# adaLN block with block attention and a routed FFN: q and k projected once per group of tokens, feature matmuls over 32 rows in two row groups

## The reference

```python
mod = silu(c) @ wmod                       # per batch: sa, ca, ga, sb, cb, gb
h = layernorm(x) * (1 + ca) + sa
q, k, v = split(h @ w_qkv.T)               # 8 heads of 16
qp = elu(q_head @ proj[head]) + 1          # 16 -> 128 features per head
kp = elu(k_head @ proj[head]) + 1
kv = kp.T @ v ;  num = qp @ kv             # inside each block of 32 tokens
out = num / (qp . sum(kp) + 1e-8)
x = x + ga * (out @ w_out.T + b_out)       # |ga|, |gb| held at 0.25 or more
h = layernorm(x) * (1 + cb) + sb
e = argmax(softmax(h @ w_red @ wg_n.T))    # one of 8 experts for each token
x = x + gb * score * (gelu(h @ w1[e] + b1[e]) @ w2[e] + b2[e])
```

## Time and profile before

| | value |
|---|---|
| runs (three) | 354.63, 355.92, 356.35 us |
| profiled execution, first to last instruction | 351.6 us |
| what lies around it (median of the runs less the span) | 4.3 us |
| setup until the first Relu of features | 14.59 us |
| step of group 0 | 26.80 us |
| steps of groups 1 and 2 (no scatter) | 20.58 and 21.66 us |
| steps of groups 3 to 6 (with a scatter) | 25.75, 29.95, 28.91, 29.05 us |
| step of group 7, to the end of its features' Exp | 22.23 us |
| tail of the routing | 36.00 us |
| expert stage | 93.08 us |
| busy: PE, ACT, DVE, POOL | 303.9, 217.3, 238.8, 157.1 us |
| mean granted TensorE clock | 0.919 |

### The profile page before, as it was taken

How to read it: one execution, slowest core, us unless ns; L and a number is a source line. 1 busy time by engine, 2 the same in 40 slices (tenths; PEclk the granted TensorE clock), 3 DMA queues, 4 the chain that set the end, 5 groups by cost and what they waited for, 6 DMA issues and landing times. The chain is left out here.

```text
span 351.6 us, 12222 instructions
## 1 busy us (share of the span) xinstructions
PE 303.9 (86%) x4080; PEld 235.6 (67%) x4081; DVE 238.8 (68%) x762; ACT 217.3 (62%) x498; POOL 157.1 (45%) x169
## 2 busy tenths in 40 slices
PE   7887999999799799789979979667869999999970
PEld 3545767777576477567757757343349999999970
DVE  3778689899778548757936958874715666666660
ACT  2478499888678459649837959311116766776740
POOL 6103513534735732661680480575503455455451
PEclk9999699999989859969967999976989999999996
DMA  6993000200220210030040022023942544444400
GB/s 168 333 311 83 0 5 2 62 5 0 85 66 1 90 60 0 35 114 0 0 149 1 2 92 62 4 91 128 281 147 67 143 118 119 131 123 115 144 26 0
DMA packets 23611, 29.53 MB, mean 84 GB/s; under 512 B 2831, under 2 KB 18451, under 8 KB 23584
## 3 DMA queue, kind: packets, MB, share of 16 engines
q1 hardware_dynamic: 19712, 19.98, 20.2%
q0 software_dynamic: 3296, 8.41, 6.6%
q10 hardware_dynamic: 576, 0.79, 0.7%
HBM read 15.32 MB, written 10.64 MB: 74 GB/s over the span
## 5 line engine op out<-in xcount | busy, mean ns | idle before, releaser
L1005 DVE SCALAR_TENSOR_TENSOR phi<-ps,ebuf 128x512 f32<-128x512 f32 x128 | 82.2, 683 | 46.5 <-ACT ebuf L494 45.9
L490 ACT ACTIVATE ebuf<-ps 128x1024 f32<-128x1024 f32 x64 | 65.5, 1024 | 36.1 <-PE ps L682 32.7
L494 ACT ACTIVATE ebuf<-ebuf 128x512 f32<-128x512 f32 x128 | 74.3, 635 | 0.1
L680 PE MATMUL ps<-hT_hi,mix_lo 128*128 (+1 forms) x128 | 63.2, 494 | 9.0 <-DVE phi L1005 5.9
L462 POOL DMA_INDIRECT out<-yo,tok x39 | 40.0, 1025 | 51.3 <-DVE yo L1311 29.0
L593 ACT ACTIVATE gT<-ps,b_cols 128x128 f32<-128x128 f32 x156 | 44.6, 368 | 21.8 <-issue 14.2
L682 PE MATMUL ps<-hT_hi,mix_hi 128*128 (+1 forms) x128 | 54.9, 429 | 0.5 <-issue 0.3
L681 PE MATMUL ps<-hT_lo,mix_hi 128*128 (+1 forms) x128 | 54.8, 428 | 0.0
L835 PE MATMUL ps<-w_sb,gT 128*128 x312 | 41.3, 275 | 0.2 <-ACT gT L593 0.2
L680 PEld LDWEIGHTS ps<-hT_hi,mix_lo 128*128 128x128 f32 x128 | 26.1, 204 | 20.2 <-DVE phi L1005 6.9
L835 PEld LDWEIGHTS ps<-w_sb,gT 128*128 128x128 f32 x312 | 38.0, 192 | 0.4 <-issue 0.4
(11 more groups left out here) (170 smaller groups left out, 476.8 us busy)
## 6 DMA issues: line engine op xcount, KB each, us to landing
rin<-sorted_rows SPq DMA_DIRECT2D x39, 192.5 KB
w1b<-in_L_ffn_w SPq DMA_DIRECT2D x1, 2048.0 KB, 13.7
rec<-h2m SPq DMA_DIRECT2D x7, 256.0 KB, 2.6
rec<-x SPq DMA_DIRECT2D x7, 256.0 KB, 2.8
sorted_rows<-pad_rec SPq DMA_DIRECT2D x5, 192.5 KB
sorted_rows<-pad_rec ACTq DMA_DIRECT2D x4, 192.5 KB
out<-yo,tok POOLq DMA_INDIRECT x39
w1b<-in_L_ffn_b SPq DMA_DIRECT2D x1, 512.0 KB, 6.7
```

The costliest lines, as they stand in the source:

```text
L490: nc.scalar.activation(ebuf[:, h % 2, :, :], x_ps[h % 2], ACT.Relu, scale=-1.0).then_inc(s_neg, 1)
L494: nc.scalar.activation(ebuf[:, h % 2, j, :], ebuf[:, h % 2, j, :], ACT.Exp, scale=-1.0).then_inc(s_exp, 1)
L680: mm(x_ps[h % 2][:, j, :], mix_lo[:, j, h, :], hi, start=True, stop=False)
L1005: v.scalar_tensor_tensor(out=phi[:, h % 4, j, :], in0=x_ps[h % 2][:, j, :], scalar=0.0, in1=ebuf[:, h % 2, j, :], op0=ALU.max, op1=ALU.add ...
```

## The change

Instead of folded weights, q and k are projected once for each group (`project_in`): two fp32 matmuls of 128 rows x 512 tokens with the transposed weights `wqkvT`. Both use the one PSUM bank `t_ps`, one after the other. ScalarE copies each out as the high part in fp32r (`keep_qk_hi`), VectorE subtracts and gives the low part (`split_lo`). GpSimd's `split_lo` and VectorE's `split_hi` go.

The feature matmuls then contract over the 16 values of a head only. A matmul takes the 32 rows of two neighbouring heads; the rows of the other head are zero in `proj_m` (times `parity`). One unit h of the loop now makes q (even h) or k (odd h) features of a pair of heads, (0,2), (1,3), (4,6) or (5,7). The six matmuls of a unit take the two heads in turn, and the two heads of a pair lie in different groups of 32 rows and go to different PSUM banks. A unit waits until both halves of the unit two before it are done; before, each half waited for its own. The scores of two heads are computed together after every second unit, and ScalarE's copy of them is one of 128x256 in place of two of 128x128.

w_qkv, w_red and w_out arrive transposed (and w_out permuted) from the host, so their transposes and copies in the setup go. SP's first load is x of group 0. In TensorE's order `turn_xn` and in ScalarE's `keep_hT` move from h=5 to h=4, `project_in` for q stands at h=5 and for k at h=6. TensorE's loop holds two steps per turn.

```diff
-            fold(0, 0)
-            fold(1, 0)
...
+            def project_in(g, j):
+                if j == 0:
+                    pe.wait_ge(s_ht, g + 1)
+                else:
+                    pe.wait_ge(s_lo, 2 * g + 1)
+                mm(t_ps, wqkvT[:, j, :], hT[:, :], start=True, stop=True).then_inc(s_qk, 1)
...
-                for j in range(2):
-                    if not (isinstance(g, int) and g == 0 and h < 2):
-                        pe.wait_ge(s_phi, 2 * (H * g + h) - 3 + j)
-
-                    mm(x_ps[h % 2][:, j, :], mix_lo[:, j, h, :], hi, start=True, stop=False)
-                    mm(x_ps[h % 2][:, j, :], mix_hi[:, j, h, :], lo, start=False, stop=False)
-                    mm(x_ps[h % 2][:, j, :], mix_hi[:, j, h, :], hi, start=False, stop=True).then_inc(s_x, 1)
+                j, heads = h % 2, PAIRS[h // 2]
+                if h < 2:
+                    pe.wait_ge(s_lo, 2 * g + j + 1)
+                if isinstance(g, int) and g == 0 and h < 2:
+                    pe.wait_ge(set_proj, 1)
+                else:
+                    pe.wait_ge(s_phi, 2 * (H * g + h) - 2)
+                for wt, mv, first, last in ((proj_lo, qk_hi, True, False), (proj_hi, qk_lo, False, False), (proj_hi, qk_hi, False, True)):
+                    for i, head in enumerate(heads):
+                        at = slice((head // 2) * BLK, (head // 2 + 1) * BLK)
+                        done = mm(x_ps[h % 2][:, i, :], wt[at, head % 2, :], mv[at, par, j, :], start=first, stop=last)
+                done.then_inc(s_x, 1)
...
+            def keep_qk_hi(g, j, first):
+                act.wait_ge(s_qk, 2 * g + j + 1)
+                if not first:
+                    act.wait_ge(s_x, H * (g - 1) - 1 + j)
+                nc.scalar.copy(qk_hi[:, bass.ds(g % 2, 1), j, :].rearrange("p a n -> p (a n)"), t_ps).then_inc(s_hi, 1)
...
+            def split_lo(g, j):
+                dve.wait_ge(s_hi, 2 * g + j + 1)
+                v.tensor_tensor(qk_lo[:, bass.ds(g % 2, 1), j, :].rearrange("p a n -> p (a n)"), t_ps,
+                                qk_hi[:, bass.ds(g % 2, 1), j, :].rearrange("p a n -> p (a n)").bitcast(F32), ALU.subtract).then_inc(s_lo, 1)
...
-            step(0, False, False, True)
-            step(1, True, False, True)
-            with pe.Fori(2, NG - 1) as g:
-                step(g, True, True, True)
-            step(NG - 1, True, True, False)
+            step(0, 0, False, False, True)
+            step(1, 1, True, False, True)
+            step(2, 0, True, True, True)
+            with pe.Fori(3, NG - 2, 2) as g:
+                step(g, 1, True, True, True)
+                step(g + 1, 0, True, True, True)
+            step(NG - 1, 1, True, True, False)
```

More of the change, by code:

```diff
@@ L684, in scores @@
-            def scores(g, h):
-                pe.wait_ge(s_phi, 2 * (H * g + h + 1))
-                if not (isinstance(g, int) and g == 0 and h == 0):
-                    pe.wait_ge(s_asb, H * g + h)
-                for t in range(TG):
-                    for c_ in range(NC):
-                        at = t * P + c_ * BLK
-                        last = mm(a_ps[c_ * BLK:(c_ + 1) * BLK, t * BLK:(t + 1) * BLK],
-                                  phi[:, h % 4, 1, at:at + BLK], phi[:, h % 4, 0, at:at + BLK], start=True, stop=True)
+                    pe.wait_ge(set_proj, 1)
+                else:
+                    pe.wait_ge(s_phi, 2 * (H * g + h) - 2)
@@ new lines, in feats, with scores @@
+                for wt, mv, first, last in ((proj_lo, qk_hi, True, False), (proj_hi, qk_lo, False, False), (proj_hi, qk_hi, False, True)):
[3 more added lines that the diff above has]
+                done.then_inc(s_x, 1)
+            def scores(g, k):
+                pe.wait_ge(s_phi, 2 * (H * g + 2 * k + 2))
+                if not (isinstance(g, int) and g == 0 and k == 0):
+                    pe.wait_ge(s_asb, NP_ * g + k)
+                for i in range(2):
+                    for t in range(TG):
+                        for c_ in range(NC):
+                            at = t * P + c_ * BLK
+                            last = mm(a_ps[c_ * BLK:(c_ + 1) * BLK, i * P + t * BLK:i * P + (t + 1) * BLK],
+                                      phi[:, k % 2 * 2 + i, 1, at:at + BLK], phi[:, k % 2 * 2 + i, 0, at:at + BLK], start=True, stop=True)
@@ L999, in features @@
             def features(g, h):
-                if not (isinstance(g, int) and g == 0 and h < 4):
-                    dve.wait_ge(s_a, H * g + h - 3)
-                for j in range(2):
-                    dve.wait_ge(s_exp, 2 * (H * g + h) + j + 1)
-                    v.scalar_tensor_tensor(out=phi[:, h % 4, j, :], in0=x_ps[h % 2][:, j, :], scalar=0.0,
-                                           in1=ebuf[:, h % 2, j, :], op0=ALU.max, op1=ALU.add).then_inc(s_phi, 1)
+                k = h // 2
+                if not (isinstance(g, int) and g == 0 and k < 2):
+                    dve.wait_ge(s_a, NP_ * g + k - 1)
+                for i in range(2):
+                    dve.wait_ge(s_exp, 2 * (H * g + h) + i + 1)
+                    v.scalar_tensor_tensor(out=phi[:, k % 2 * 2 + i, h % 2, :], in0=x_ps[h % 2][:, i, :], scalar=0.0,
+                                           in1=ebuf[:, h % 2, i, :], op0=ALU.max, op1=ALU.add).then_inc(s_phi, 1)
             def keep_values(g, c, first):
@@ L1203, in step @@
                             norm2_moments(g - 1)
+                    if h == 6 and nxt:
+                        split_lo(g + 1, 1)
                     if h == 7:
```

219 lines of the change are left out of this document (94 added, 125 removed).

## The result

The changed kernel takes 387.02 us (385.13 to 389.86, four runs) against 355.27 for the kernel before beside it: ratio 1.093, 95% interval 1.085 to 1.102. The forecast was 346.9 and a gain. The profiled execution has a span of 386.7 us in place of 351.6, 35.1 more, at a mean granted clock of 0.755 in place of 0.919.

What follows compares the result with a forecast made beforehand. TensorE was taken to set the pace, ScalarE and VectorE 2 us behind. Gains of 3.0 (setup), 0.5, 5.0 and 0.5 (steps 3 to 7) made 9.0 off the 351.6 span; plus 4.3 around it, 346.9 us, range 337 to 362.

Steps and rivals of the forecast that it cites:

- Features 12.0 to 6.6 us: TensorE's 48 feature matmuls per step at full clock: overlapping row groups take 5.4 us off.
- Scores' copy 0.37, subtraction 0.69, ScalarE 20.0, VectorE 20.3: Per step: each 128x256 copy 0.37 us, each PSUM subtraction 0.69; busy sums ScalarE 20.0, VectorE 20.3.
- Steps 1 and 2 unchanged (0): Full-clock steps of 20.58 and 21.66 us: no gain, since ScalarE and VectorE are last instead of TensorE.
- stall of k's projection: k's projection waits for VectorE's low part of q, holding unit 7: 0.5 us of stall at full clock.
- scores' wait: ScalarE's copy of the scores, behind gate and project_out, ends about 0.35 us later at each: 0.7 us.
- Half clock shorter in steps 4 to 6 (-5.0): Cheaper feature units in half-clock stretches after scatters: 1.7 us gained in each step, 5.0 in all.
- clock case: Rival: TensorE's gaps spread half clock to ordinary steps, say 60 us more, costing 13 us: 360; chance 0.25.
- argument against it: Against spreading half clock: TensorE has no idle time there, so the clock comes back; units are cheaper than before.
- Setup -3.0: Setup and group 0: x loaded first, no folding, shorter features in the first four units: 3.0 us less.
- PSUM Bottleneck: Skill passage: tiling speeds TensorE, not the emptying of PSUM; by it alone the gain would be nothing.

Runs made afterwards that it cites:

- rows64: The changed kernel with the two heads of a unit in row groups of 64 rows in place of 32: 369.2 us, ratio 1.049.
- streams2: Matmul streams alone, without the kernel, with gaps and from half clock; 32-row pairs ran at 0.50 from about 66 us until the 128-row stream.
- two_banks: rows64 with scores ahead of gate and project_out, `turn_xn` to k's low part one unit later, and k projected into `m_ps`: 354.8 us, ratio 1.013.
- two_banks_flat: two_banks with TensorE's loop of two steps written out: 351.2 us, ratio 1.006.

## Why the prediction was wrong

The forecast had -9.0 us, the profiles show +35.1. From the changed kernel's 387.0, rows of 64 give 17.9, the order and the second bank 14.4 together, the loop written out 3.6: 351.2, about the kernel before. In ratios that is 1.093, 1.049, 1.013, 1.006. Two steps failed: the clock was taken to come back, and the waits of steps 1 and 2 were priced too low. By the prediction's own steps:

- *Features 12.0 to 6.6 us* held. Pairs stand 0.23 apart (0.24 taken). The Trainium skill's 3.07 times for four row tiles (TensorE: Matmul & The Clock Gate, Part 3, Measured speedup vs the span model) is less than a long stream gives here: four groups passed 320 matmuls in 18.44 us, 0.058 each against 0.229 for 128 rows, 3.97 times. At half clock a unit took 1.57 us (174.87 to 176.44), not 1.3.
- *Scores' copy 0.37, subtraction 0.69, ScalarE 20.0, VectorE 20.3*: 0.369, 0.681, 20.2 and 19.4 in step 1. These were sound. A projection took 1.12 at full clock, not 0.95.
- *Steps 1 and 2 unchanged (0)* failed: +6.6 and +5.1. Three terms were mis-sized. The stall of k's projection was put at 0.5 us a step; TensorE's two waits for low parts are 1.8. The scores' wait was to grow by 0.7; it grew by 1.9, from 0.6 to 2.5. And the move of `turn_xn`, which stands in the description of the change, was priced at nothing; it is 2.35 us a step of waiting for GpSimd. These stand on two engines and don't add up to the step. I added work by engine and looked at each wait alone, and no step followed the whole chain from xn over hT, q, its copy and subtraction, k, its copy and subtraction to unit 1 and `values`. By rows64 1.7 and 1.9 us of the excess were the clock, which fell in these steps too (0.79 and 0.78); order and two banks then gave 2.1 and 2.3. The rest, 2.8 and 0.8, stays open.
- *Half clock shorter in steps 4 to 6 (-5.0)* failed: they took 12.2 us more, of which the loop (below) is 6.5 and the clock a large part. The clock case came, to which the forecast gave a chance of 0.25. Its price was about right, 13 us for 60 or 0.22 a us, against 0.17 to 0.19 measured by rows64; its extent wasn't, 132 us more in place of 60. The argument against it, that TensorE has no idle time at half clock and so the clock comes back, is what the runs refute: pairs over 32 rows ran 54 us at half clock without idle time and didn't bring it back (streams2).
- *Loop*: the body of two steps was read and not priced. It is 6.5 us of step 4 in the changed kernel, 3.6 us of the time in two_banks.
- *Setup -3.0*: +1.8 up to step 1. hT was in time; the half clock came already there.
- *PSUM Bottleneck* (the Trainium skill, TensorEngine Tiling), which spoke against a gain, agrees with the last version. In steps 1 and 2 of two_banks_flat TensorE is busy 36.4 us where it was 40.4, ScalarE and VectorE 40.2 and 40.1 of 44.2, TensorE stands 5.3 for phi, and the time is about that of the kernel before.

## What to carry to other kernels

Shortening TensorE's work by matmuls over fewer rows can cost it the clock: try 64 rows before 32, and read the granted clock, not only the busy share. A product that is split through a copy and a subtraction is a chain across three engines; count it end to end, and give two of them two PSUM banks before moving them about in the queues, since a moved wait is only handed on. And look at the place where a loop comes round: a body of two steps in place of one can make the jump back stand.
